# Attention stack rows spread over the partitions, the maxima's band copied with heads outermost, a 128-row token tile, and expert units moved, in a one-core embed, attention and mixture kernel

## The reference

```python
# token mixing: x is (8, 64, 256, 4)
q, k, v = proj(Wq_w, Wq_b), proj(Wk_w, Wk_b), proj(Wv_w, Wv_b)
ew = jnp.exp(w_bias * local_mask); ek = jnp.exp(k)
num = jnp.einsum('ts,nsd->ntd', ew, ek * v); den = jnp.einsum('ts,nsd->ntd', ew, ek)
h = (jax.nn.sigmoid(q) * num / den) @ out_w + out_b + _flatten(x)      # then LayerNorm * ln_g + ln_b
h = jnp.concatenate([h, jnp.take(W_E, tokens, axis=0) * scale], axis=1)
# attention on LayerNorm(h); rel_logits is nonzero only within 4 tokens of the diagonal
attn_weights = jnp.einsum('btd,bsd->bts', q, k) + _rel_to_abs(jnp.einsum('btd,md->btm', q, rel_k[0]))
attn_probs = jax.nn.softmax(attn_weights, axis=-1)
out = einsum('bts,bsd->btd', attn_probs, v) + einsum('btm,md->btd', _abs_to_rel(attn_probs), rel_v[0])
h = h + out @ Wo + bo
# experts on LayerNorm(h): all 8 are computed, weights w from a router
h = h + einsum('bte,betd->btd', w, einsum('beti,eid->betd', silu(gate) * up, Wd))
```

## Time and profile before

| | |
|---|---|
| time, median of 3 runs | 1299.91 us (1299.55 to 1302.32) |
| the profiled execution's own time | 1299.13 us |
| its span in the trace | 1297.3 us |
| period of a pass with both items | 150.3 us |
| PE busy | 1109.1 us, 85% |
| DVE / ACT / POOL busy | 748.5 / 369.6 / 233.8 us |
| mean granted TensorE clock | 0.93 of full |

### The profile page before, as it was taken

The page is one execution under the profiler, slowest core; times in us unless marked ns, Lnnn a source line. Parts: engine busy times, 40 slices in busy tenths (PEclk is TensorE's granted clock), DMA queues, the critical chain, the costliest instruction groups (busy, mean ns, idle before and its releaser), DMA issues.

```text
span 1297.3 us, 16627 instructions
## 1 busy us (share of the span) xinstructions
PE 1109.1 (85%) x5668; PEld 787.9 (61%) x5668; DVE 748.5 (58%) x1579; ACT 369.6 (28%) x599; POOL 233.8 (18%) x258
## 2 busy tenths in 40 slices
PE   5537699988999798988999888998989889997798
PEld 4312288636885387745886267853877358862688
DVE  7326455674547655485556745486565846477343
ACT  1203512053220723035120531217221441206211
POOL 5314320032200402013200312004020122004000
PEclk9657879989899989999899999999999998999899
DMA  7594205602093111912056020921129020640200
GB/s 212 159 170 143 38 5 94 134 10 54 1 167 60 26 37 40 166 31 37 17 92 135 9 54 0 172 56 39 24 56 170 10 48 6 115 113 2 50 1 13
DMA packets 126846, 89.68 MB, mean 69 GB/s; under 512 B 67847, under 2 KB 116360, under 8 KB 126378
## 3 DMA queue, kind: packets, MB, share of 16 engines
q1 hardware_dynamic: 126408, 88.05, 33.3%
q0 software_dynamic: 384, 1.05, 0.3%
HBM read 60.36 MB, written 28.71 MB: 69 GB/s over the span
## 4 chain that ended last, share of the span: by engine, by line
PE 40%; issue 22%; DVE 16%; DMA 10%; SPq 5%; ACT 4%; POOL 3%; POOLq 0%; DVEq 0%; ACTq 0%
PE S L893 10%; DMA scratch<-d_band_t 6%; PE S L914 6%; PE S L767 5%; PE S L759 4%; DVE S L1202 4%; PE S L824 4%; PE S L723 3%; DVE maxima L1181 3%; PE S L807 3%; SPq L551 3%; ACT scratch L1011 3%; PE S L640 2%; DMA txt_row<-in_L_txt_W_E,txt_idx 1%; DMA w_d<-in_L_ffn_Wu 1%
## 5 line engine op out<-in xcount | busy, mean ns | idle before, releaser
L1449 POOL TENSOR_TENSOR bands<-scratch,one 64x432 f32<-64x432 f32 x128 | 119.1, 931 | 565.2 <-ACT scratch L1011 560.1
L1181 DVE TENSOR_REDUCE maxima<-S 128x2 f32<-128x768 f32 x192 | 175.6, 953 | 74.0 <-PE S L767 73.2
L914 PE MATMUL S<-w_d,hT 128*128 128x256 f32 x768 | 184.4, 388 | 1.4 <-DVE hT L1323 0.7
L1048 ACT ACTIVATE silu<-S 128x384 f32<-128x384 f32 x128 | 62.8, 491 | 411.2 <-PE S L893 331.4
L1202 DVE TENSOR_TENSOR S<-S,bands 64x144 f32<-64x144 f32 x384 | 154.4, 402 | 33.6 <-PE S L807 22.6
L759 PE MATMUL S<-k_st,q_st 128*128 128x384 bf16 x384 | 134.4, 350 | 45.0 <-DMA scratch<-d_band_t 29.8
L1011 ACT ACTIVATE scratch<-S 128x768 f32<-128x768 f32 x192 | 155.5, 811 | 44.9 <-DVE S L1202 37.3
L914 PEld LDWEIGHTS S<-w_d,hT 128*128 128x128 f32 x768 | 147.8, 195 | 23.8 <-issue 2.3
L767 PE MATMUL S<-scratch,ident_b 128*128 128x132 bf16 (+1 forms) x384 | 154.0, 401 | 0.0
L1323 DVE TENSOR_TENSOR hT<-silu,S 128x384 f32<-128x384 f32 x128 | 70.7, 552 | 125.5 <-PE S L893 119.9
L807 PE MATMUL S<-q_st,k_st 128*128 128x384 bf16 x384 | 93.1, 341 | 36.1 <-ACT scratch L1011 34.8
(11 more groups left out here) (157 smaller groups left out, 1478.0 us busy)
## 6 DMA issues: line engine op xcount, KB each, us to landing
bands<-d_band_s SPq DMA_DIRECT2D x16, 864.0 KB, 9.1
scratch<-d_band_t SPq DMA_DIRECT2D x8, 1632.0 KB, 16.8
d_parts<-scratch SPq DMA_DIRECT2D x48, 192.0 KB, 2.0
q_st<-d_parts SPq DMA_DIRECT2D x48, 192.0 KB
k_st<-d_parts SPq DMA_DIRECT2D x48, 192.0 KB
d_band_w<-bands SPq DMA_DIRECT2D x32, 240.0 KB, 3.8
out<-scratch SPq DMA_DIRECT2D x8, 384.0 KB, 2.5
x_in<-in_x SPq DMA_DIRECT2D x8, 256.0 KB, 3.5
```

The lines of the kernel that those rows point to most:

```text
L914: mm = pe.matmul(D[:, i // 2, (i % 2) * E:(i % 2 + 1) * E], hT[:, (FT * e + m) % 3, i * P:(i + 1) * P], w_d[:, e, m, :], start=(m == 0), s ...
L1181: dve.tensor_reduce(dst, S[:, c0:c0 + 2, PAD:PAD + T], AX, ALU.max).then_inc(max_done.sem, 1)
L1449: nc.gpsimd.tensor_tensor(bands[rows, :, :, 2 * pair:2 * pair + 2].rearrange("p i w h -> p h i w"), win, one[rows].unsqueeze(2).unsqueeze( ...
```

## The change

It does seven things.

1. **Stack rows.** `d_parts` is laid out as 128 rows of 768 numbers, and slot n of a stack fills the 16 partitions 2+n, 10+n, ... 122+n, each by one run of 6144 numbers. Rows 0 and 1 hold the maxima. The columns of w_q and w_k are permuted to fit (four DVE copies, once), and `rel_k`, the biases and embedding columns too.
2. **Band.** A copy `band_h` of `band_t` has the heads ahead of the token offset, so that one head is contiguous. The first two heads are copied by DVE at the head of `maxima`, the other seven pairs by ACT, one at every third item. PE waits for each.
3. **Token tile.** `x_in`, `wkv`, `wq_t` and `resid` have 128 rows; rows 65 to 127 are zero, from four memsets at the start. `x_in` keeps its layout of token by head.
4. **Small loads.** The eight loads of the embedding columns become one from DRAM, and the mask `head_of_row` is not loaded; three small DRAM-to-DRAM transfers reorder the biases and the embedding.
5. **Zeroing.** Of `d_band_w` only the two ends are zeroed.
6. **Units.** After `project_v` 15 instead of 20; in `maxima` 8 instead of 5; after `negate` 3 instead of 2; after `turn_attn` 6 instead of 5.
7. POOL zeroes all 128 rows of the stacks rather than 32, once.

```diff
-FILL_MAXIMA = [0, 0, 0, 1, 0, 0, 0, 1, 0, 0, 0, 1, 0, 0, 0, 1, 0, 0, 0, 1, 0, 0, 0, 0]
+FILL_MAXIMA = [0, 0, 1] * 8
...
-FILL_NEGATE = 2
-FILL_OUT = [("turn_outputs", 3), ("turn_attn", 5), ("turn_weights", 1), ("rel_values", 1)]
+FILL_NEGATE = 3
+FILL_OUT = [("turn_outputs", 3), ("turn_attn", 6), ("turn_weights", 1), ("rel_values", 1)]
...
-        wkv = sb("wkv", [F + 1, 2 * F])
-        wq_t = sb("wq_t", [F + 1, F])
-        resid = sb("resid", [F + 1, H, F])
+        wkv = sb("wkv", [P, 2 * F])
+        wq_t = sb("wq_t", [P, F])
+        resid = sb("resid", [P, H, F])
...
-        x_in = sb("x_in", [F + 1, L, H])
+        x_in = sb("x_in", [P, L, H])
...
+        band_h = Z[:, 0:TT * ROWB // 2].bitcast(BF16).rearrange("p (i h w) -> p i h w", i=TT, h=AH)
...
                 def stack(st, base, order):
                     for n in range(SLOTS):
                         sp.dma_start(
-                            st[AD * n:AD * (n + 1)],
-                            d_parts[base + order[n]].rearrange("(h d) t -> d h t", d=AD)
+                            st[NEG + n:P:G8].rearrange("p h t -> p (h t)"),
+                            d_parts[base + order[n]].rearrange("(d g) m t -> d (g m t)", d=AD)
                         ).then_inc(stacked.sem, 16)
...
-                    pe.wait_ge(band_t_in.sem, band_t_in.at(b, 1))
...
+                if n == 0:
+                    pe.wait_ge(band_first.sem, band_first.at(b, 1))
+                elif n % 3 == 0:
+                    pe.wait_ge(band_turned.sem, band_turned.at(b, n // 3))
...
-                                       band_t[rows, i, w0:w1, h],
+                                       band_h[rows, i, h, w0:w1],
...
+            def maxima(b, n):
+
+                if n == 0:
+                    act.wait_ge(band_t_in.sem, band_t_in.at(b, 1))
+                pair = n // 3 + 1
+                if n % 3 == 0 and pair < AH // 2:
+                    heads = slice(2 * pair, 2 * pair + 2)
+                    nc.scalar.activation(band_h[:, :, heads], band_t[:, :, :, heads].rearrange("p i w h -> p i h w"),
+                                         ACT.Copy).then_inc(band_turned.sem, 1)
...
             def maxima(b, n):
+                if n == 0:
+                    dve.wait_ge(band_t_in.sem, band_t_in.at(b, 1))
+                    dve.tensor_copy(band_h[:, :, 0:2], band_t[:, :, :, 0:2].rearrange("p i w h -> p i h w")
+                                    ).then_inc(band_first.sem, 1)
```

More of the change, by code:

```diff
@@ L1057, in _ @@
         def _(dve):
+            for part in (wkv, wq_t, resid, x_in):
+                dve.memset(part[F:P], 0.0).then_inc(rows_zero, 1)
+            dve.wait_ge(rows_zero, 4)
+            dve.memset(x_in[F:F + 1], 1.0).then_inc(ones_ready, 1)
             dve.memset(bands[:], 0.0).then_inc(zero_ready, 1)
[L1060 removed]
             dve.memset(spare[:, 2:3], 0.0).then_inc(stored.sem, 16)
```

92 lines of the change are left out of this document (57 added, 35 removed).

## The result

The changed kernel takes 1259.12 us in the median of four runs (1256.37 to 1263.92), the kernel before 1300.7 (1299.55 to 1302.32). The ratio is 0.968, with a 95% interval of 0.965 to 0.972: faster, by 41.6 us. The profiled execution took 1256.37 us, its span is 1254.5.

What follows compares the result with a forecast made beforehand. PE's timeline was taken to set the pass: the fill before `maxima`, `maxima`, and the mixing steps. Terms summed to -6.4 us a pass, -45 for seven, +4 for the first pass: 1259 us, range 1237 to 1279.

Steps and rivals of the forecast that it cites:

- Stacks and the start of `maxima` (-5.3): Fill before `maxima`: faster stack transfers and five fewer units let PE start at 837.1 against 842.4, -5.3 us a pass.
- The geometric mean, 223 GB/s: Rate taken for the twelve stack transfers, between today's 144 GB/s and `band_t`'s 346; they then last 10.6 us.
- `maxima` (-1.7): In `maxima`: band matmul at 0.08 us without its step, 27.0 us instead of 28.7 with three units more inside.
- ACT's copy: In `maxima`: ACT's band copies take 0.9 us each, a pair every third item, and lie in ACT's idle time.
- After `negate` (+1.3): Between turned maxima and `attend`: a gate, an up and a first half, 3.85 us instead of 2.59; +1.3 us.
- at the end (+0.9): After `turn_attn`: the sixth unit is not hidden, so PE carries +0.9 us in this stage.
- Token tile (-1.6): Mixing steps: with 128 rows the clock no longer falls, so L675's eight matmuls take 1.79 us; -1.6 us a pass.
- The rival with the clock as before (0.25): Mixing steps: the clock falls as before, seven passes lose 11 us of gain, 1270 us; chance 0.25.
- priced at nothing: Token tile: zero rows leave the pace of the `x_in` loads unchanged, because the step of four numbers stays; 0 us.
- The rival that the rows were the brake of the loads (0.12): Token tile: `x_in` loads speed up with 128 rows, -2.8 us a pass more, 1239 us; chance 0.12.
- The first pass (+4): First pass: maxima items wait for ACT's copies behind weight rounding, +2, extra w_q and w_k copies some 2; +4 us (-3 to +9).
- 8 us earlier at most: First pass: loads come at most 8 us earlier, so the weights' rounding ends at 98.5 instead of 106.4.

Runs made afterwards that it cites:

- e5: Changed kernel with each stack transfer filling 16 neighbouring partitions instead of 16 set eight apart, run lengths the same; 1333.5 us.
- e6: Changed kernel with 32 unused numbers behind each row of 384 in `d_parts`, so that runs are 768 bytes instead of 12 KB; 1286.6 us.
- e3: Changed kernel with only the unit table put back to that of the kernel before (20 units after `project_v`, five in `maxima`); 1260.8 us.
- e1: Changed kernel without the band copies: PE reads `band_t` with its step of 16 numbers again; 1283.4 us.
- e2: Changed kernel with the token tile's matmuls taking the first 65 rows instead of 128, buffers, memsets and steps the same; 1279.1 us.
- e10: Changed kernel reading `x_in` as if heads lay one behind the other, without the step of four numbers; output not the reference's; 1242.4 us.
- e7: Changed kernel with the three reordering transfers of single numbers issued behind the load of `x_in`; 1264.4 us.
- e8: As e7, and POOL's memsets of the stacks also wait for DVE's copies at the start; 1254.2 us.
- e4: Changed kernel, first pass: ACT makes band copies before rounding the weights' second half, SP issues Wd last, PE waits for weights at the end; 1249.6 us.
- e11: Changed kernel with e8 and e4, second-half rounding behind the last band copy, 16 units after `project_v` and two after `negate`; 1265.2 us.
- e12: Changed kernel with e8's start, e11's first pass, POOL laying out `x_in` without a step, 16 units after `project_v`, none behind `maxima`'s third item; 1223.9 us.

## Why the prediction was right, step by step

**Stacks and the start of `maxima` (-5.3).** From the turn of the norm to the first product it was 36.99 us and is 31.68: -5.3. The geometric mean, 223 GB/s, met the 222 of the trace; it was a choice between two rows far apart, so that it met is luck. The landing came 17.2 us after the first issue (17.6 in the sum), and DVE's copy took 1.12 us where I took 0.9, behind two accumulations, as described. e5 and e6 show that the partitions did nearly all of the faster landing. The -5.3 is that and the five units moved out of the way, together: in e3, where they stay, this stretch is 36.5 us, and the gain shows in `maxima` (25.2 us) and behind it, with the same period.

**`maxima` (-1.7).** 28.7 to 27.0. The band matmul passes in 0.055 us, under the 0.08 that I took and at my lower bound of 0.06; a triple with a unit takes 3.23 us (forecast 3.2). e1 shows the cause. One term was mis-sized without harm: ACT's copy takes 1.69 us and not 0.9, but only the first pass waits for it.

**After `negate` (+1.3) and at the end (+0.9).** Turned maxima to `attend`: 2.92 us before, 4.17 now, +1.25. From the turn of the outputs to the next opening 19.75 before, 20.61 now, +0.86.

**Token tile (-1.6).** The eight matmuls take 1.89 us, and the stretch up to the turned norm is 1.76 us shorter. The rival with the clock as before (0.25) fell, and with it the rule of the Trainium skill on which I had it rest (TensorE: Matmul & The Clock Gate, What's actually happening), read as one that doesn't see rows: in e2 and in the changed kernel PE is busy for all of the 3.70 us ahead of the fall (3.79 us for the sixteen in both). That zero rows left the pace of the loads alone held too. But "priced at nothing" was only right for this edit: e2 shows that, with the falls in `attend`, the rows are worth 20 us and not 11. The rival that the rows were the brake of the loads (0.12) fell as well, and e10 shows the step as the brake; the prediction named the step as what differs, but not what its removal is worth.

**Sum.** The terms measured in this pass are -5.3, -1.7, +1.25, +0.86, -1.76 and -0.35 in `attend` (28.06 to 27.71, not forecast): -7.0, against -6.4. The mean over the seven is -7.2, since the kernel before had passes of up to 151.9 us. Its parts, in the same order, are -5.2, -1.7, +0.6, +0.8, -2.0 and +0.4 in `attend`. So the example pass was not typical in two places. In passes 1, 2 and 7 the kernel before took 4.3 to 4.4 us from the turned maxima to `attend`, not 2.92. And with the clock at 1.00 its `attend` took 26.5 us and not 28.06: `attend` did not gain, it lost, mostly by the 0.79 (in the last pass, with the clock at 1.00, it took 26.9).

**The first pass (+4) was mis-sized:** +7.9. By stages it is +8.6 at the opening, -11.1 from there to the first product, +9.0 to `attend` and +1.4 behind. The sum had the loads "8 us earlier at most" and priced the small loads at nothing, as "under work that waits for DVE". The last rounding ends at 103.5 us, 3.0 earlier than before and not 8, so PE waited for ACT until 105 and not 99. And the small loads cost something: three transfers of single numbers stood ahead of `x_in`, and the added memsets pushed DVE's cast into POOL's memset (e7, e8), 8.6 us at the opening. Of that the steps up to the turned norm took up 3.7: they had waited for DVE before. The wait for ACT's copies was placed rightly; from the first product to `attend` the pass is 9.0 us longer, and e4 and e11 get it back.

The errors of +3.9 and of 7 times -0.8 cancelled but for 2 us, and the rest is the spread of the runs: the profiled execution took 1256.4, the median is 1259.1. That it met 1259 to the tenth is luck; that the stacks, the band and the token tile each gave about what was forecast is not.

## What to carry to other kernels

Look for small steps in what PE reads: 16 bytes in a float operand, or 32 in a bf16 one, doubled to quadrupled a matmul here, and an idle engine's copy removed it. A transfer to few partitions is best judged by where they lie, before its run length. And after every gain on PE read the granted clock of all later stretches, pass by pass: here it took back 8.5 us of e4's gain over three passes, and 3.4 us in every pass of e12. Read more than one pass of the kernel before, too.

## What was not expected of the hardware

- Rows of zeros made a difference to the clock: with 65 rows the granted clock fell in the mixing steps of each pass 1 to 7 (0.56 in the window shown), with 128, of which 63 are zero, in none.
- The same instructions run at different clocks from pass to pass. e8's `attend` has 0.76 and 0.82 in pass 2 and 0.79 and 1.00 in pass 3; a head start of 6.3 us was down to 0.5 after three passes. What it is worth to save a microsecond in this kernel can't be told from that place alone.
- An fp32 matmul of 128 columns passes in 0.12 us when its loaded operand has no step and 0.24 with a step of four numbers; 132 bf16 columns in 0.055 and 0.22 (16 numbers).
- DVE's cast of 512 columns took 0.42 us alone and 5.08 beside a 5.2 us memset of POOL.
- ACT copies 816 bf16 numbers with a step of 16 in 1.69 us, DVE in 1.12, though both cast 768 fp32 numbers to bf16 without one in 0.84 (ACT) and 0.56 (DVE).
- A wait of PE that was 1.2 to 1.9 us longer at the head of `maxima` (e6) went with a clock of 0.57 in the 4 us behind it, in the pass shown; behind the changed kernel's wait of 1.15 us it is 1.00, but 0.58 in its last pass with both items, where the wait was 1.96.
